# Attention rounds on TensorE: the matmuls of the negated maxima moved ahead of the late maximum

## The reference, cut to what matters

```
# N_HEADS = 16, HEAD_DIM = 64; here b = 1, s = 2048
q = (x @ Wq).reshape(b, s, N_HEADS, HEAD_DIM)
k = (x @ Wk).reshape(b, s, N_HEADS, HEAD_DIM)
v = (x @ Wv).reshape(b, s, N_HEADS, HEAD_DIM)
dot = jnp.einsum('bihd,bkhd->bhik', q, k)
w = jax.nn.softmax(dot / jnp.sqrt(jnp.float32(HEAD_DIM)), axis=-1)
a = jnp.einsum('bhij,bjhd->bihd', w, v)
return a.reshape(b, s, N_HEADS * HEAD_DIM) @ Wo + bo
```

## Time and profile before

| What | us |
|---|---|
| Median of three runs | 2028.22 (2026.49 to 2033.28) |
| The profiled execution's own time | 2027.76 |
| Its span, first to last instruction | 2026.2 |
| PE busy in the span | 1797.5 (89%) |
| DVE busy | 1422.3 (70%) |
| POOL busy | 1148.9 (57%) |
| ACT busy | 799.9 (39%) |

### The profile page before, as it was taken

How to read it: one execution, slowest core, us unless ns; L and a number is a source line. 1 busy time by engine, 2 the same in 40 slices (tenths; PEclk the granted TensorE clock), 3 DMA queues, 4 the chain that set the end, 5 groups by cost and what they waited for, 6 DMA issues and landing times.

```text
span 2026.2 us, 29341 instructions
## 1 busy us (share of the span) xinstructions
PE 1797.5 (89%) x10570; PEld 992.3 (49%) x10570; DVE 1422.3 (70%) x2371; ACT 799.9 (39%) x1239; POOL 1148.9 (57%) x741
## 2 busy tenths in 40 slices
PE   5988874294899999999999999999999999995893
PEld 4766654282444444444444444444444444443383
DVE  4566656335787778777787778777787788776564
ACT  3344342062344444444444444444444444442131
POOL 2344430403477777677776777777777777783302
PEclk8898995596999999999999999999999999997897
DMA  7000000121000000000000000000000000003112
GB/s 237 1 1 1 1 1 1 34 63 29 1 1 1 1 1 1 1 1 1 1 1 1 1 1 1 1 1 1 1 1 1 1 1 1 1 1 96 32 54 62
DMA packets 41510, 32.38 MB, mean 16 GB/s; under 512 B 3604, under 2 KB 37392, under 8 KB 41368
## 3 DMA queue, kind: packets, MB, share of 16 engines
q1 hardware_dynamic: 31096, 22.12, 3.6%
q0 software_dynamic: 2048, 4.20, 0.7%
q10 hardware_dynamic: 8224, 4.19, 0.7%
HBM read 18.96 MB, written 11.53 MB: 15 GB/s over the span
## 4 chain that ended last, share of the span: by engine, by line
PE 73%; issue 4%; DVE 4%; POOL 3%; ACT 1%; DMA 1%; DVEq 0%; POOLq 0%; ACTq 0%
PE psum L1601 23%; PE psum L1586 20%; PE psum L1560 8%; PE psum L1580 5%; PE psum L1227 2%; PE psum L1616 2%; PE psum L1610 2%; PE psum L1001 2%; PE psum L1533 1%; PE psum L1013 1%; PE psum L1187 1%; DVE a_mx L1765 1%; PE psum L1237 1%; POOL x_rows L780 1%; PE psum L1535 1%
## 5 line engine op out<-in xcount | busy, mean ns | idle before, releaser
L1897 POOL TENSOR_TENSOR a_acc<-a_acc,a_Pb 128x832 f32<-128x832 f32 x448 | 894.9, 1998 | 305.3 <-ACT a_Pb L1703 272.6
L1765 DVE TENSOR_REDUCE a_mx<-psum 128x2 f32<-128x1024 f32 x512 | 625.6, 1224 | 235.6 <-PE psum L1560 232.6
L1703 ACT ACTIVATE a_Pb<-psum 128x1024 f32<-128x1024 f32 x512 | 496.8, 1022 | 701.1 <-PE psum L1586 701.1
L1601 PE MATMUL psum<-a_Pb,a_Vb 128*64 128x512 f32 x2048 | 494.1, 603 | 0.0
L1816 DVE TENSOR_TENSOR a_acc<-a_acc,a_Pb 128x192 f32<-128x192 f32 x448 | 232.0, 518 | 28.9 <-ACT a_Pb L1703 5.4
L1601 PEld LDWEIGHTS psum<-a_Pb,a_Vb 128*64 128x64 f32 x2048 | 127.0, 136 | 244.6 <-issue 173.4
L1560 PE MATMUL psum<-a_Kh,a_Qh 64*128 64x512 f32 x1024 | 230.7, 446 | 8.1 <-DVE a_mx L1765 8.1
L1586 PE MATMUL psum<-a_Qh,a_Kh 64*128 64x512 f32 x1024 | 230.5, 445 | 0.0
L1560 PEld LDWEIGHTS psum<-a_Kh,a_Qh 64*128 64x128 f32 x1024 | 96.7, 184 | 222.1 <-issue 211.2
L1586 PE MATMUL psum<-a_Ql,a_Kh 64*128 64x512 f32 x1024 | 203.3, 392 | 0.0
L1586 PE MATMUL psum<-a_Qh,a_Kl 64*128 64x512 f32 x1024 | 202.5, 390 | 0.0
(11 more groups left out here) (374 smaller groups left out, 2173.1 us busy)
## 6 DMA issues: line engine op xcount, KB each, us to landing
x_rows<-zero ACTq DMA_DIRECT2D x2, 2048.0 KB, 21.7
g_w<-in_L_ffn_w_eDF_dram SPq DMA_DIRECT2D x2, 1408.0 KB, 8.8
r_W<-in_L_ffn_W_dram SPq DMA_DIRECT2D x1, 2048.0 KB, 12.4
r_tile_x<-x_rows SPq DMA_DIRECT2D x16, 128.0 KB, 2.1
y_rows<-r_tile_y SPq DMA_DIRECT2D x16, 128.0 KB, 1.8
g_tile_x<-x_rows SPq DMA_DIRECT2D x16, 128.0 KB, 2.2
y_rows<-g_tile_y SPq DMA_DIRECT2D x16, 128.0 KB, 1.8
g_w<-in_L_ffn_w_eFD_dram SPq DMA_DIRECT2D x2, 512.0 KB, 10.7
```

Of the source, the lines that this page charges most:

```text
L1601: last = pe.matmul(ps[HEAD[h], B_O, :], b.Vb[:, p // 2 % 2, kc, at], b.Pb[:, step % BUFS, h * QT:(h + 1) * QT], start=(kc == 0), stop=(kc ...
L1703: act.activation(b.Pb[:, step % BUFS, :], ps[:, slot:slot + 2, :].rearrange("p a b -> p (a b)"), ACT.Exp, scale=SCALE).then_inc(S["probs"], 1)
L1765: v.tensor_reduce(b.mx[:, :, qc, quarter:quarter + 1], ps[:, bank:bank + 2, :], AX.X, ALU.max).then_inc(S[f"free{bank}"], 1)
L1897: g.tensor_tensor(b.acc[:, u, at], before, b.Pb[:, step % BUFS, at], ALU.add).then_inc(S["added_pool"], 1)
```

## The change

`scores` is split in two. `below_max(R)` takes the wait for the mask, the wait for the exponentials of the round before and the four matmuls of the negated maxima; `scores(R)` keeps the waits for queries and keys and the products. In the loop `below_max(R)` stands first, ahead of the late maximum. No instruction is added or removed but for waits; DVE, ACT and POOL keep their order.

```diff
-    def scores(R):
+    def below_max(R):
         U, d = R // RN, R % RN
-        p = U // NU
         if d == 0:
             freed(("mask", U))
-            freed(("q", U))
-            freed(("k", p, NU - 1))
         if R:
             pe.wait_ge(S["probs"], 2 * R)
         for g in range(4):
             rows = slice(32 * g, 32 * (g + 1))
             pe.matmul(ps[:, 2 * (g % 2) + g // 2, :], b.ones[rows, :], b.Mr[rows, :], start=True, stop=False, tile_position=(32 * g, 0))
+
+    def scores(R):
+        U, d = R // RN, R % RN
+        p = U // NU
+        if d == 0:
+            freed(("q", U))
+            freed(("k", p, NU - 1))
         for i in range(2):
...
     for R in range(ROUNDS):
         late, early = max_jobs(R - 1)[1], max_jobs(R)[0]
+        below_max(R)
         if R and late:
             maximum(*late[1:])
         scores(R)
```

## The result

The changed kernel takes 2116.76 us (median of four runs, 2112.16 to 2121.76), the kernel before 2030.75 beside it (2026.49 to 2035.95): a ratio of 1.0435, 95% interval 1.0407 to 1.0464. Slower, as forecast; the forecast size was 3.8%, the measured one is 4.4%. The profiled execution took 2112.16 us and its span is 2110.6, so 84.4 us more than before, where the sum said 76.1.

What follows compares the result with a forecast made beforehand. PE was taken to set the pace, as long as DVE's reductions came in time. 17.2 + 58.9 = 76.1 us on the profiled 2027.76 gave 2104 us, slower by 3.8%; range 2045 to 2125.

Steps and rivals of the forecast that it cites:

- One change of tile less: PE, late maximum and products now share a tile: taken alone 0.19 us a round, 47 us off over 246 rounds.
- The reduction takes it back: DVE's reduction between the two maxima needs 1.93 us, PE leaves 1.74: early maximum stays at 2.36, the gain lost in full.
- The reload: PE, early maximum released late loads its weights late: 0.08 us a round in 215 rounds, 17.2 us on.
- The unit's end: In d == 7 POOL catches DVE's second add, delaying the mask; PE loses 1.9 us at 31 ends, 58.9 us on.
- The clock: PE's clock at stops of 1.8 us: falls, 141 us more, only a rival; chance 0.10 together with more caught adds.
- third sign of being wrong: The prediction is wrong if PE's clock shows falls between 600 and 1700 us in the profile after.
- Rival 1: DVE's second add at the unit's end gets in ahead of POOL: 24 us on, 2052 us; chance 0.20.
- Rival 2: The reduction does not hold the early maximum, the saved tile change stands: 47 us off, 1981; chance 0.05 for faster.
- Rival 3: More adds caught in ordinary rounds, 2222 us, or the clock falls at units' ends, 2245 us; chance together 0.10.
- What would show it: Signs in the profile after: early maximum still at 2.36, many short `a_mx` waits, some 30 `a_Mr` waits of 1.8 us.

Runs made afterwards that it cites:

- e4: Changed kernel, with DVE's reduction of each late maximum reading only half its columns: 2033.66 us against 2025.14 for the kernel before, ratio 1.0041.
- e9: e4 with DVE's adds of rounds d == 6 and 7 removed, deferred ones done in the next d == 0 and 1: 1983.46 us against 2021.22, ratio 0.9811.
- e5: Kernel before, with the reduction of each late maximum halved: 2028.91 us against 2025.14, ratio 1.0008.
- e1: Changed kernel, with the old order restored in the rounds d == 7 alone: 2053.11 us against 2031.27 for the kernel before, ratio 1.0131.
- e3: Changed kernel, with DVE's two adds of each round d == 7 moved to the next round: 2052.31 us against 2031.27 for the kernel before, ratio 1.0112.
- e8: Changed kernel, with one POOL add per round d == 7 cut to 8 columns from 832: 2050.32 us against 2031.27 for the kernel before, ratio 1.0094.
- w1: New order except in d == 7, ACT copying half of each late maximum for DVE to reduce later, adds as in e9: 2011.07 us against 2021.22, ratio 0.9962.

## Why the prediction was right, point by point

- **One change of tile less** is worth 0.19 us. Right: e4 and e9 show 0.17 to 0.25 in each of the seven rounds, and e5 that it is not the shorter reduction by itself. A slip in the sum: 0.77 + 6 x 0.23 is 2.15, not 2.17 (e4 has 2.14), so the lack was 0.21 rather than 0.19. It changes nothing that follows.
- **The reduction takes it back.** Right: the early maximum came 2.34 behind the weighing's end where 2.36 was computed, and was released as soon as the reduction was made shorter.
- **The reload**, 0.08 a round. Mis-sized a little: the seven rounds lost 0.66 together, 0.094 each, so some 20 us where the sum had 17.2 (it counted 215 rounds where there are 216). The next group comes 0.43 behind the held maximum, not 0.41. e1, where it is almost alone, costs 22 us.
- **The unit's end**, 1.9 us in 31 places, 58.9. Mis-sized: 1.78, so 55. DVE's second add asked 0.28 after POOL's start (0.29 computed) but ended 2.20 after that start, where 2.35 was computed: POOL's add was hardly pushed back by DVE's first one. I had it begin its 2.0 us when DVE's add ended; it ran from its own start and took 1.99, its pair 4.07. That e3 and e8, which have in common only that they take the catch away, both end at 2050 to 2052 shows the cause.
- **The clock.** This is the step that failed in the sum, which put it at nothing. "A stop of 1.38 left it at 1.00" was made the measure for a stop of 1.8, and the fall was put among the rivals with 0.10. The clock fell behind 9 of the 31 ends and cost 1.2 us each, 11 us, far less than the 4.55 a unit that was priced. Six of the falls lie between 600 and 1700 us, so the prediction's own third sign of being wrong did come. That the stops bring them on is supported by e1, e3 and e8, where the stops at the units' ends are gone and the clock does not fall in the stage, and by all 13 traces together: after its start the stage has 20 falls, each with a stop of 1.62 us or more, and none with any of the 104 stops of 1.0 to 1.51 us. Yet 29 stops of 1.62 us or more, one of 3.37 among them, had no fall; why stays open.
- **The total.** Part of its closeness is luck. The reload cost 3 us more than the sum had and the units' ends 4 less; the clock cost 11 more, and the other stages were 3 us shorter in the profiled execution, which nobody had forecast. Together that is most of the way from 76.1 to the measured 84.4.
- **Rival 1** (the add gets in) named 2052 for a kernel in which it does; e3 and e8 made it come about and measured 2052.31 and 2050.32. Against the kernel before beside them that is 21 and 19 us, where 24 was computed. **Rival 2** (the saved change stands) was excluded by 1.93 against 1.74; e9 fulfils its condition. **Rival 3**, catches in inner rounds, cost PE time in three rounds of the changed kernel (0.27, 1.17 and 1.16 us; the kernel before has two, 1.5 and 1.9), and one unit's end had both adds caught, the stop of 3.37. With rounds shorter by another 0.3 (e4, w1) they came in every unit or in every one from 24 on. Its other half, the clock, is above.
- **What would show it**: "waits for `a_mx` are many and short" was wrong for that view, which counts 11; the hold is visible in the distances alone.

## What to carry to other kernels

Before work is moved on the engine that sets the pace, compute for each shared buffer the time from its filling to its next filling and set it against what the reader needs: the wait until it starts, its own length and the release (here 1.74 against 1.93). What a new order saves below that need comes back as a wait. Then look one engine further: a hand-over that starts 0.44 us later can meet another engine's instruction that it used to pass by a tenth. Where two engines hinder each other, list when each is busy by round and place the work in the pauses; that and a second engine on the hand-over made the new order, kept in seven rounds of eight of units 0 to 23, 1.8% faster instead of 4.4% slower.

## What the runs showed of the hardware

- A DVE add with both inputs in SBUF that starts while POOL's add runs ends some 0.2 us after POOL's, whatever its own length: 1.91 instead of 0.36. In the kernel before, 117 of 118 such adds ended 0.21 to 0.33 us behind POOL's; the other one began in the same 0.01 us as POOL's add and took 0.36. The reduction and the mask, which read PSUM, kept 1.21 and 0.67 beside the same POOL adds (1051.45 and 1052.58 in the changed kernel). The Trainium skill, SBUF — State Buffer, section SBUF: two separate sides, states it as an exclusive lock on a shared port pair, held for the whole instruction by whichever starts first. The trace agrees, and e8 shows that shortening the holder is enough. It goes the other way too: in the kernel before, POOL's add at 1018.61 found DVE's normalisation running to 1019.02 and took 2.25 instead of 1.96.
- Between groups on tiles of 64*128 and of 32*128 the first group after the change comes 0.43 after the one before it, and the next 0.34; on the same tile it is 0.23. The change from the early maximum to the weighing (128*64) shows 0.33. An early maximum that was held by a semaphore delays its successor by 0.08 to 0.1 us besides its own wait (0.41 and 0.43 instead of 0.33).
- After 9 of the 29 stops of 1.62 to 1.64 us in the changed kernel, each between stretches of dense matmuls, the granted clock was 0.50 for 3.4 us, and each cost 1.2 to 1.3 us.
